# Range checks of register loads left out in the first expert stage of a two-layer kernel

## What is computed

```python
x = hidden_states.reshape(-1, 128)                 # layer-normalised tokens
scores = sigmoid(x @ gate_w.T)                     # 32 experts
_, topk_ids = top_k(scores + e_bias, 4)            # each token goes to 4 of them
topk_w = take_along_axis(scores, topk_ids, axis=1)
topk_w = topk_w / sum(topk_w, axis=1)
g = einsum('th,ehi->tei', x, w1)                   # 96 hidden columns per expert
u = einsum('th,ehi->tei', x, w3)
a = silu(g) * u * combine[:, :, None]
out = einsum('tei,eih->th', a, w2)
```

## Time and profile before

| | before |
| --- | --- |
| median of three runs | 995.78 us |
| lowest and highest | 994.69, 996.07 us |
| span of the profiled execution | 992.6 us |
| TensorE matmul busy | 639.3 us, 3898 instructions |
| TensorE weight load busy | 398.8 us |
| VectorE busy | 623.1 us |
| ScalarE busy | 423.5 us |
| GpSimd busy | 379.0 us |
| mean granted TensorE clock | 0.820 of full |

### The profile page before, as it was taken

One profiled execution on the slowest core, in us unless ns is written; L12 is line 12 of the kernel. 1 busy time (PEld: TensorE's weight loads), 2 busy tenths in 40 slices (PEclk: granted clock), 3 DMA queues, 4 the chain that ended last, 5 costly groups with the idle time before them and its releaser, 6 DMA issues.

```text
span 992.6 us, 14085 instructions
## 1 busy us (share of the span) xinstructions
PE 639.3 (64%) x3898; PEld 398.8 (40%) x3927; DVE 623.1 (63%) x1579; ACT 423.5 (43%) x906; POOL 379.0 (38%) x345
## 2 busy tenths in 40 slices
PE   4487887776658361778781636777763221899991
PEld 2243343243224240577650313343432111787881
DVE  2678998878948887257533633877755667343443
ACT  2484866676758231344440213443542000343442
POOL 2314223554361388000016887183420000665641
PEclk9997996897979666699995677988996555899996
DMA  5795875564545022244423311000002000111115
GB/s 148 231 309 178 291 255 176 170 205 154 181 175 174 9 83 79 78 125 122 117 79 112 137 42 38 1 16 1 12 10 97 0 0 1 44 41 40 44 32 138
DMA packets 82754, 102.84 MB, mean 104 GB/s; under 512 B 11317, under 2 KB 66169, under 8 KB 82298
## 3 DMA queue, kind: packets, MB, share of 16 engines
q1 hardware_dynamic: 58618, 80.04, 25.1%
q0 software_dynamic: 6592, 13.51, 4.5%
q10 hardware_dynamic: 17472, 8.39, 2.9%
HBM read 82.25 MB, written 19.66 MB: 103 GB/s over the span
## 4 chain that ended last, share of the span: by engine, by line
PE 35%; DVE 32%; ACT 8%; issue 7%; POOL 6%; DMA 6%; another core or an unknown queue 4%; SPq 2%; ACTq 0%; DVEq 0%; POOLq 0%
POOL xs L585 4%; DVE oh L1176 4%; PE PS L1981 4%; DMA oh<-index 4%; DVE nmx L1313 3%; PE PS L1959 3%; PE PS L1964 3%; PE PS L1789 2%; PE PS L1890 2%; PE PS L1972 2%; PE PS L1781 2%; DVE pkr L1140 2%; DVE pk L1189 1%; DVE ctok L1167 1%
## 5 line engine op out<-in xcount | busy, mean ns | idle before, releaser
L617 POOL DMA_INDIRECT yb<-ys,yrow x64 | 61.5, 960 | 139.8 <-DMA ys<-y 117.8
L1176 DVE TENSOR_SCALAR oh<-oh,pcol 128x2048 bf16<-128x2048 bf16 x80 | 75.1, 939 | 26.6 <-DMA oh<-index 25.6
L585 POOL DMA_INDIRECT xs<-xn,row x64 | 78.5, 1226 | 32.3 <-issue 18.6
L1692 PE MATMUL PS<-oh,T 128*128 128x512 bf16 x211 | 67.4, 425 | 27.2 <-ACT oh L778 24.4
L580 POOL TENSOR_TENSOR vv<-vv,coef 128x1280 f32<-128x1280 f32 x16 | 44.4, 2772 | 98.1 <-DVE coef L1160 89.1
L683 POOL DMA_INDIRECT xg<-xrows,tok x39 | 37.5, 962 | 107.6 <-DVE tok L1522 96.0
L1697 PE MATMUL PS<-oh,T 128*32 128x512 bf16 x960 | 76.2, 422 | 1.9 <-issue 1.8
L1706 PE MATMUL PS<-ident,gs 128*128 128x128 f32 x320 | 56.8, 304 | 23.5 <-ACT vv L799 22.8
L1313 DVE TENSOR_REDUCE nmx<-PS 128x4 f32<-128x616 f32 x64 | 48.8, 793 | 27.5 <-remote 18.5
L777 ACT ACTIVATE oh<-oh,pcol 128x512 bf16<-128x512 bf16 x80 | 57.7, 721 | 15.5 <-DMA oh<-index 15.5
L1706 PEld LDWEIGHTS PS<-ident,gs 128*128 128x128 f32 x320 | 36.6, 151 | 62.0 <-issue 48.3
(11 more groups left out here) (370 smaller groups left out, 1729.6 us busy)
## 6 DMA issues: line engine op xcount, KB each, us to landing
oh<-index SPq DMA_DIRECT2D x80, 512.0 KB
oh<-index SPq DMA_DIRECT2D x80, 128.0 KB
x<-xs SPq DMA_DIRECT2D x96, 64.0 KB, 1.9
ys<-y ACTq DMA_DIRECT2D x48, 128.0 KB, 2.2
w0r<-in_w SPq DMA_DIRECT2D x8, 384.0 KB, 5.8
xs<-nil SPq DMA_DIRECT2D x8, 256.0 KB
wg1r<-in_wg SPq DMA_DIRECT2D x1, 2048.0 KB
wu1r<-in_wu SPq DMA_DIRECT2D x1, 2048.0 KB
```

The source lines that it names most:

```text
L585: pool.indirect_dma_start(xs[:], bass.IndirectOffsetOnAxis(ap=row0[:, QT * b + t, k:k + 1], axis=0), xn1[:, b % 2, t, :], None).then_inc(s ...
L617: pool.indirect_dma_start(yb[:, b % 2, t, k, :], None, ys[:], bass.IndirectOffsetOnAxis(ap=yrow0[:, QT * b + t, k:k + 1], axis=0))\
L1176: dve.tensor_scalar(main, main, pcol[:, 0:1], None, ALU.is_equal).then_inc(s["oh_main"], 1)
L1692: pe.matmul(o, T2[:, b % 2, p, n // NK, :], oh[:, slot, GH, :], start=(p == 0), stop=False, skip_group_check=True)
```

## The change

Two loads get an argument that leaves out the check of each loaded value against its least and greatest value at run time. The bounds themselves stay given for the addresses. A constant holds the reason as a text; an unused constant goes. The other loads of this kind (lines 490, 819 and 1947) are not touched.

```diff
-GAP_EXPERTS = 0
+TABLE_IN_RANGE = "the tile table is made on the chip: row sums of tile counts bounded by the shapes, and an expert held to the last one"
...
             def load_tile(i):
                 if i % 4 == 0:
-                    _, rows4[:] = nc.values_load_multi_w_load_instructions(tabi[0:1, 0, i:i + 4], [mybir.EngineType.SP], min_val=0, max_val=XS_ROWS - P)
+                    _, rows4[:] = nc.values_load_multi_w_load_instructions(tabi[0:1, 0, i:i + 4], [mybir.EngineType.SP], min_val=0, max_val=XS_ROWS - P,
+                                                                              skip_runtime_bounds_check_because=TABLE_IN_RANGE)
                 sp.dma_start(x0[:, i % XB0, :], xs[bass.ds(rows4[i % 4], P)]).then_inc(s["tile_in%d" % (i % XB0 // 2)], 16)
...
             def experts_of(m):
-                _, e = nc.values_load_multi_w_load_instructions(tabi[0:1, 1, 2 * m:2 * m + 4], [mybir.EngineType.PE], min_val=0, max_val=E0 - 1)
+                _, e = nc.values_load_multi_w_load_instructions(tabi[0:1, 1, 2 * m:2 * m + 4], [mybir.EngineType.PE], min_val=0, max_val=E0 - 1,
+                                                              skip_runtime_bounds_check_because=TABLE_IN_RANGE)
                 return list(e)
```

## The result

The kernel after takes 967.95 us, the median of four runs (964.39 to 973.01 us), against 995.77 us (994.69 to 996.07 us) of the kernel before beside it: a ratio of 0.9733 [0.9685, 0.9782]. Two later comparisons of the same pair, on two chips (0 and 3), gave 0.9762 [0.971, 0.9814] and 0.9739 [0.9682, 0.9796]. A ratio here is that of all the runs and not of the two medians, so it can differ from their quotient by a few thousandths. The forecast of 974.0 us was a ratio of 0.9781, at the upper edge of the first interval. By the ratios, carried over to 995.8 us, 24 to 27 us were won (by the medians 22 to 28 us), where 21.8 us had been forecast.

The account below looks back on a forecast made before the run. TensorE in the first expert stage, held up by range checks on its register loads, was taken as the bound. 19.6 us at full clock plus 2.15 us at the start gave 21.8 us: 995.8 to 974 us, range 969 to 980.

Parts of the forecast that it names:

- What bounds the kernel: First expert stage: TensorE is nearest to a bound, yet idles before line 1781 (15.1 and 6.2 us) behind line 1752's checks.
- The price of a load's checks: TensorE's load of four expert numbers, line 1752: its four checks hold the sequencer for 1.13 us at full clock.
- The six pieces: VectorE's row-number work, even iterations 16 to 26: loses its cover, delays x0l, costs 6 x 0.69 = 4.1 us.
- Rival B: The six pieces of row numbers cost nothing, so 4.1 us more are won: 970 us; chance 0.13.
- The start: Start of the first expert stage: SP's first checks 1.03 us, TensorE's "issue" 0.28 us, transposes at 404.67 0.34 us sooner.
- The number of loads at the full clock: Of 24 loads on TensorE, 21 run at full clock; iteration 1 brings 0.5 us, iteration 3 nothing.
- The 0.2%: About 2 us is what a measurement of this kernel can tell from no change.
- rival C: Stores of y become the bound, VectorE waiting for the store three pairs back: 984 us; chance 0.09.
- rival E: TensorE's granted clock falls in the busier expert stage and the kernel gets slower: 1036 us; chance 0.04.
- The queue of TensorE: Skill's 64-deep queue would hide checks; forecast held they show in full, with some 25 instructions an iteration and waits for x0l.

Follow-up runs that it names:

- the repeat of after: The changed kernel, unchanged, run again for a second profile: 977.11 us (six runs) against 999.22 us of the kernel before, 0.9762.
- small pieces: Row-number work cut from six pieces into 24 over iterations 16 to 39, on top of the changed kernel: 964.26 us, 0.9701; once more 930.99 us, 0.9722.

## Why the prediction was right, and where it was not

*What bounds the kernel.* Right. The 21 us before line 1781 were neither h nor "issue" but the four checks ahead of it: without them they are 0.2 us, and with TensorE's checks alone gone the stage is 18.8 us shorter, with SP's alone 0.5 us, both against the second profile of before.

*The price of a load's checks, 1.13 us.* Right: 2.79 to 1.66 us in an iteration, and 0.28 us per check in steps of two and four.

*The six pieces, 4.1 us.* Right in kind, place and size: 2.35 us in these iterations, x0l as the wait, 0.60 us where 0.6 to 0.7 was written, and 2.35 - 1.65 = 0.70 us each, 4.2 us for six. Cut small, the pieces gave back 3.7 to 3.8 us in these six iterations on two chips; the whole stage, where the clock rose early, became only 1.8 to 3.1 us shorter, mostly because the register load took longer in five iterations. Rival B is out.

*The start: 1.03, 0.28 and 0.34 us.* Right: the chain of after has no check between SP's load and its first address, and TensorE's "issue" of 0.34 us is 0.04 us. The transposes of iterations 0 and 1 come 0.30 and 0.40 us sooner behind the ones before them than in the second profile of before (1.91 to 1.61 and 2.03 to 1.63 us). With SP's checks alone gone the second step is 1.62 us too, so the 0.34 us were SP's, as written.

*The number of loads at the full clock.* This was the mis-sized term. The sum took 21 hot loads, 0.5 us in iteration 1 and nothing in iteration 3, because in the profile of before the clock was at the half level until 416 us. For a stage with a late clock that is right, as the rows above show (0.49 us and nothing). But late was the rare case: two of thirteen profiles. In the second profile of before the clock rose 7.7 us into the stage, in the three of after 5.4 us. There iteration 3 brings its full 1.13 us, and the sum is 21.8 + 1.13 = 22.9 us, a ratio of 0.9770. In iteration 1 the checks bring 0.54 us, as forecast, and the clock, which rose earlier in after, about 0.5 us more; whether this half belongs to the change is open. With it the sum is 23.4 us, a ratio of 0.9765. The three comparisons gave 0.9733, 0.9762 and 0.9739, each with an interval that takes in both, and the forecast's 0.9781 as well, so the times alone do not show the error; the rows of iterations 1 to 4 do. The intervals reach half a per cent (5 us) to either side. The 0.2% that the forecast held to be enough was not.

*How the first pair's 28.9 us are made up.* 23.6 us in the expert stage (22.1 us against the second profile of before, so 1.5 us of it is the late clock), 1.03 us ahead of its first transfer and 5.8 us in the attention, which is chance; the rest of the kernel took 1.5 us more. Against the second profile of before the change's own part is 22.1 + 1.0 = 23.1 us, 23.7 us with the repeat of after and 24.2 us with its third profile. Row by row the first of these stages adds up: 16.9 us in the 15 loads without a piece (16.95 forecast), 2.9 in the six with one (2.64; before had longer loads there), 1.1 in iteration 3, 1.0 in iteration 1, 0.7 in the two iterations ahead of it and 0.2 in the others, less 0.8 us at the stage's end, which is 22.1 us with rounding. The lower median of the first comparison, 967.95 us, isn't explained by the change: the same kernel had 977.11 us in the repeat, on a chip where before had 999.22 us.

*The stores of y (rival C)*. Its mechanism appeared, and nearly nothing hung on it. VectorE waits for a store once in the first profile of after (1.7 us, at the end) and three times in each of the two others (1.5 us together): 0.9 to 1.0 us at the end, and twice 0.2 to 0.4 us in the loop. The iterations in which the two loop waits of the second profile fall are not longer than their neighbours of the same kind (1.71 for 1.70 us). What it cost is at most 0.8 us at the end of the first profile; it did not bound the loop. *The clock (rival E)*. The whole stage has 0.97 with TensorE 94% busy, and the missing 3% (2 x 0.03 x 88.2 = 5.3 us at the half level) are those of its first 16 us (5.4). From 418.87 us on it is 1.00. It did not fall.

*The queue of TensorE.* Checks were hidden in the second expert stage of this kernel (114.6 without against 114.2 us with) and laid bare in the first, where the lead of the sequencer comes out as an estimated 0.27 us. The Trainium skill, "TensorE: Matmul & The Clock Gate", section "Architectural detail: the array is 16× 32×32, not 1× 128×128", gives a queue 64 deep, by which checks would hide under queued work: the second stage agrees with it, the first does not. An iteration of the first has 28 matmuls and weight loads (674 matmuls in 48 iterations, and as many loads), where the forecast counted some 25. That the sequencer's stops at semaphore waits keep its lead so short is argued from the code. The second stage has such waits in each of its tiles too, and what sets the lead there was not tried.

*What the range rests on.* The expert's number is held to 31 by an instruction. The first row is not, although the kernel's description says "kept": no instruction limits it. It is 128 times the tile's number plus a sum of `skip` (lines 1222 and 1224 of the kernel before), at most 95 x 128 plus 32 regions, which is XS_ROWS - P, so the shapes bound it.

*Open.* The iterations with a load that took 1.9 to 2.1 us in after are those whose register load was long: 516 ns in the one of 1.92 us, 575 ns in that of 2.01 us and 608 ns in the 2.09 us of the repeat, against 329 to 343 ns in those of 1.66 us. What makes such a load long isn't known. The lead of 0.27 us is worked out from after and fits the iterations shown of the four kernels with other checks or loads within 0.03 us. For the long loads it gives 0.1 to 0.2 us too little, and it was not measured by itself. The variants with two checks and with one-sided checks had one run each, and their verdicts rest on the rows.

## What to carry to other kernels

A register instruction that no busy time counts can be the bound: if an engine idles just behind one and the profile names "issue" or a tile that was long ready, look at the source view of the line with the register load. Its price is the sequencer's time (0.28 us for each two-sided check here) less the lead that the sequencer has over its engine; where that engine is full, as in the second expert stage, it is nothing. When it goes, ask what was hidden under it (six pieces here, 0.70 us each) and whether another engine with the same burden is next (SP, 3.3 us). Leave a check out only where something else holds the value in its range, as the minimum and the shapes do here.

A term that hangs on a state at one moment, as the loads at the half clock did, wants a second profile, or bounds that take in both states.

## What the hardware showed that was not expected

A register load of two values took 722 ns (529 to 887), of four values 332 ns (328 to 575, up to 608 in the repeat) and, in line 1947, of one value 301 ns. More values were not dearer, and two were the dearest; what makes it so was not tried. The same load of four values took over 500 ns in none to five of the 22 cases from iteration 3 on, by profile; in after and its repeat such a case lengthened its iteration by 0.3 to 0.4 us.

TensorE's granted clock fell to the half level at times in the middle of the expert stage in one kernel, the one with a load in each iteration (0.89 from 470 to 515 us, with 245 matmul instructions there against 285 of before in the same stretch), while in after, with TensorE busy for 94% of the stage, it did not fall. Why it fell is not known. The kernel before showed 7.7 and 14.7 us at the half level at the start of the stage, in two executions; small pieces showed 5.1 and 14.1 us, with 3.0 us of stage time between the two.
